# Low-rank expert matrices of the last stage: all eight experts' factors against the two chosen ones fetched by index

## What is computed

```python
def _gates(cls_tok, Wr):
    logits = cls_tok @ Wr.T
    top_vals, top_idx = jax.lax.top_k(logits, K)          # K = 2 of E = 8
    ...
    return jax.nn.softmax(masked, axis=-1)
gates = _gates(x[:, 0, :], Wr)
mid = jnp.einsum('blh,erh->belr', x, A)                   # A: 8 x 64 x 256
expert_out = jnp.einsum('belr,ehr->belh', mid, Bw)        # Bw: 8 x 256 x 64
weighted = jnp.einsum('be,belh->blh', gates, expert_out)
return x + weighted
```

## Time and profile before

| | before |
|---|---|
| median of 3 runs | 502.54 us (502.24 to 504.96) |
| the profiled execution, its own time | 502.1 us |
| its span in the trace | 500.3 us |
| TensorE busy in the span | 471.9 us, 94% |
| VectorE, ScalarE, GpSimd busy | 285.4, 202.6, 234.0 us |
| 480 to 490 us of the span: TensorE busy | 10.00 of 10.00 us |
| 490 to 501 us: TensorE busy | 6.95 of 11.00 us |
| granted TensorE clock, 440 us to the end | 1.00 |

### The profile page before, as it was taken

How to read it: one execution, slowest core, us unless ns; L and a number is a source line. 1 busy time by engine, 2 the same in 40 slices (tenths; PEclk the granted TensorE clock), 3 DMA queues, 4 the chain that set the end, 5 groups by cost and what they waited for, 6 DMA issues and landing times.

```text
span 500.3 us, 9491 instructions
## 1 busy us (share of the span) xinstructions
PE 471.9 (94%) x3132; PEld 387.1 (77%) x3132; DVE 285.4 (57%) x656; ACT 202.6 (40%) x453; POOL 234.0 (47%) x312
## 2 busy tenths in 40 slices
PE   6899999798999999989999999999977999899897
PEld 5677776575777787769999999999965777677686
DVE  3879985642263122345555545454564689998733
ACT  3455774556620021002323232323323666665640
POOL 3523344044237566129985643333327655662350
PEclk9999999998999999999999999999997999999999
DMA  8999300020002224999223323221129100000004
GB/s 275 363 427 362 27 12 1 1 85 2 0 1 89 89 90 129 333 331 309 45 61 97 105 86 86 66 86 54 43 88 315 41 0 1 1 3 1 1 23 146
DMA packets 48879, 53.51 MB, mean 107 GB/s; under 512 B 15265, under 2 KB 43234, under 8 KB 48578
## 3 DMA queue, kind: packets, MB, share of 16 engines
q1 hardware_dynamic: 35890, 24.33, 17.4%
q0 software_dynamic: 7424, 19.67, 11.6%
q10 hardware_dynamic: 5520, 8.91, 5.9%
HBM read 35.78 MB, written 17.12 MB: 106 GB/s over the span
## 4 chain that ended last, share of the span: by engine, by line
PE 77%; DVE 12%; ACT 4%; DMA 3%; issue 2%; ACTq 1%; POOL 1%; SPq 0%; POOLq 0%
PE banks L1212 10%; PE banks L1262 9%; PE banks L1314 5%; PE banks L347 5%; PE banks L325 5%; PE banks L361 5%; PE banks L1315 5%; PE banks L1318 5%; PE banks L314 3%; DVE mx L503 3%; PE banks L1336 3%; PE banks L1337 3%; PE banks L1340 3%; PE banks L1728 3%; PE banks L1326 3%; DVE ps L506 2%
## 5 line engine op out<-in xcount | busy, mean ns | idle before, releaser
L116 POOL TENSOR_TENSOR rstd<-var,mhalf 128x2 f32<-128x2 f32 x30 | 21.0, 698 | 92.8 <-DVE var L109 92.8
L1142 ACT ACTIVATE hg<-banks 128x352 f32<-128x352 f32 x39 | 18.1, 465 | 96.6 <-PE banks L1318 91.8
L1314 PE MATMUL banks<-w_hi,xgT_hi 128*128 x156 | 54.8, 352 | 2.0 <-ACT xgT_hi L949 1.9
L1487 DVE TENSOR_TENSOR hgT_lo<-banks,hgT_hi 128x256 fp32r<-128x256 f32 x78 | 24.1, 351 | 56.2 <-ACT hgT_hi L1149 56.2
L503 DVE TENSOR_REDUCE mx<-banks 128x16 f32<-128x1024 f32 x32 | 39.0, 1220 | 24.5 <-PE banks L325 24.4
L1315 PE MATMUL banks<-wd,xgT_hi 128*128 x156 | 50.3, 324 | 0.0
L1262 PE MATMUL banks<-sdn,big 128*128 128x256 f32 x192 | 47.5, 393 | 0.0
L1262 PEld LDWEIGHTS banks<-sdn,big 128*128 128x128 f32 x192 | 34.1, 189 | 12.6 <-issue 9.0
L325 PE MATMUL banks<-kvb,qT 64*128 64x256 f32 x256 | 37.6, 414 | 4.0 <-DVE ps L506 2.9
L1046 POOL DMA_INDIRECT expert_rows_in<-xn,slot x32 | 31.5, 986 | 18.3 <-issue 7.6
L1318 PE MATMUL banks<-w_hi,xgT_lo 128*128 x156 | 37.6, 322 | 0.0
(11 more groups left out here) (244 smaller groups left out, 1140.3 us busy)
## 6 DMA issues: line engine op xcount, KB each, us to landing
w_hi<-in_egu POOLq DMA_DIRECT2D x2, 2816.0 KB, 21.1
expert_rows_in<-zeros SPq DMA_DIRECT2D x1, 5304.0 KB, 40.0
xn<-expert_rows_in SPq DMA_DIRECT2D x39, 128.0 KB, 2.0
y_all<-choices_out SPq DMA_DIRECT2D x16, 256.0 KB, 5.5
wd<-in_egu ACTq DMA_DIRECT2D x8, 352.0 KB, 9.5
wd<-in_egu ACTq DMA_DIRECT2D x4, 704.0 KB, 13.5
out_x<-x SPq DMA_DIRECT2D x8, 256.0 KB, 2.1
x<-in_x SPq DMA_DIRECT2D x2, 896.0 KB, 8.1
```

Source lines behind the costliest of these rows:

```text
L1314: nc.tensor.matmul(to, xgT_hi[:, c, k, :], hi, start=(k == 0), stop=False)
```

## The change

The factors are no longer loaded whole. `choose` works out, for each of 128 partitions, a row number: partitions 0 to 63 hold the 64 rows of the first chosen expert, partitions 64 to 127 those of the second (`kmax` is 8 minus the expert's number, so the row is 512 - 64 * `kmax` + the partition's place in its half). GpSimd then fetches these rows of both factors for each batch by four indirect DMAs. The gates need only two halves of one column. With 128 rows in place of 512, a batch's matrix takes 2 matmuls and its weighting one instruction. The order is changed too: both weightings and both matrices stand at slot 16 with the first unit's product, both `keep_matrix` stand right behind `inverse(7)` on ScalarE, and `turn3(5)` comes after `project_o(7)`.

```diff
 def top_two(nc, dve, sem, base, p, rev, work, shape, low):
-    key, top1, hot1, rest, top2, hot2, kmax = work
+    key, top1, hot1, rest, top2, hot2, kmax1, kmax2 = work
...
-    for src, top, hot in ((p, top1, hot1), (rest, top2, hot2)):
+    for src, top, hot, kmax in ((p, top1, hot1, kmax1), (rest, top2, hot2, kmax2)):
...
-        fa = space("fa", KR * D).rearrange("p (k n) -> p k n", k=KR)
-        fb = space("fb", KR * D).rearrange("p (k n) -> p k n", k=KR)
-        fbg = space("fbg", B * KR * D).rearrange("p (b k n) -> p b k n", b=B, k=KR)
+        fa, fb, fbg = [space(n, B * D).rearrange("p (b n) -> p b n", b=B) for n in ("fa", "fb", "fbg")]
...
-            nc.tensor.wait_ge(ffn1_in, 48)
+            nc.tensor.wait_ge(ffn1_in, 16)
...
             v.tensor_tensor(gc["d"][:, :], gc["top2"][:, :], gc["top1"][:, :], ALU.subtract).then_inc(f_g, 1)
+            nc.vector.wait_ge(f_rows, 2)
+            for q, kmax in enumerate(("kmax1", "kmax2")):
+                half = slice(q * R, (q + 1) * R)
+                link(v.scalar_tensor_tensor(gc["row"][half, :], gc[kmax][half, :], -float(R), first_row[half, :], ALU.mult, ALU.add))
+            v.tensor_copy(picked[:, :], gc["row"][:, :]).then_inc(f_rows, 1)
...
             link(v.reciprocal(gc["inv"][:, :], gc["den"][:, :]))
-            wide = lambda a: a.unsqueeze(2).to_broadcast([P, B, E])
-            link(v.tensor_tensor(gt["gate"][:, :, :], gt["hot2"][:, :, :], wide(gc["e"][:, :]), ALU.mult))
-            link(v.tensor_tensor(gt["gate"][:, :, :], gt["gate"][:, :, :], gt["hot1"][:, :, :], ALU.add))
-            link(v.tensor_tensor(gt["gate"][:, :, :], gt["gate"][:, :, :], wide(gc["inv"][:, :]), ALU.mult))
-            for b in range(B):
-                pairs = gt["gate"][:, b, :].rearrange("p (k q) -> p k q", q=2)
-                for q in range(2):
-                    v.tensor_copy(gcol[q * R:(q + 1) * R, b, :], pairs[q * R:(q + 1) * R, :, q]).then_inc(f_gcol, 1)
+            v.tensor_copy(gcol[0:R, :], gc["inv"][0:R, :]).then_inc(f_gcol, 1)
+            v.tensor_tensor(gcol[R:2 * R, :], gc["inv"][R:2 * R, :], gc["e"][R:2 * R, :], ALU.mult).then_inc(f_gcol, 1)
+
+        def first_rows():
+            nc.gpsimd.iota(first_row[:, :], [[0, B]], base=E * R, channel_multiplier=1,
+                           allow_small_or_imprecise_dtypes=True).then_inc(f_rows, 1)
+
+        def second_half_rows():
+            nc.vector.wait_ge(f_rows, 1)
+            v.tensor_scalar(first_row[R:2 * R, :], first_row[R:2 * R, :], -float(R), None, ALU.add).then_inc(f_rows, 1)
+
+        def pick_factors(b):
+            nc.gpsimd.wait_ge(f_rows, 3)
+            for to, table in ((fa, a_in), (fb, bw_in)):
+                nc.gpsimd.indirect_dma_start(to[:, b, :], None, table[:, :],
+                                             bass.IndirectOffsetOnAxis(ap=picked[:, b:b + 1], axis=0),
+                                             bounds_check=E * R - 1).then_inc(f_picked[b], 16)
 
         def weigh_second_factor(b):
-            nc.scalar.wait_ge(f_gcol, 2 * B)
-            nc.scalar.wait_ge(ffn1_in, 48)
-            for k in range(KR):
-                nc.scalar.activation(fbg[:, b, k, :], fb[:, k, :], ACT.Copy, scale=gcol[:, b, k:k + 1]).then_inc(f_scaled, 1)
+            nc.scalar.wait_ge(f_gcol, 2)
+            nc.scalar.wait_ge(f_picked[b], 32)
+            nc.scalar.activation(fbg[:, b, :], fb[:, b, :], ACT.Copy, scale=gcol[:, b:b + 1]).then_inc(f_scaled, 1)
 
         def batch_matrix(b):
-            nc.tensor.wait_ge(f_scaled, (b + 1) * KR)
+            nc.tensor.wait_ge(f_scaled, b + 1)
             wait(nc.tensor, events1["sub_done"], 2 * NU)
             for m in range(KD):
-                for k in range(KR):
-                    last = nc.tensor.matmul(MATRIX_IN[b][:, m * D:(m + 1) * D], fa[:, k, m * P:(m + 1) * P],
-                                            fbg[:, b, k, :], start=(k == 0), stop=(k == KR - 1))
+                last = nc.tensor.matmul(MATRIX_IN[b][:, m * D:(m + 1) * D], fa[:, b, m * P:(m + 1) * P],
+                                        fbg[:, b, :], start=True, stop=True)
             last.then_inc(f_w, 1)
...
             sp.dma_start(wr[:, :, :], split(wr_in)).then_inc(ffn1_in, 16)
-            sp.dma_start(fa, a_in.rearrange("(k p) n -> p k n", p=P)).then_inc(ffn1_in, 16)
-            sp.dma_start(fb, bw_in.rearrange("(k p) n -> p k n", p=P)).then_inc(ffn1_in, 16)
...
-                       16: lambda: (batch_matrix(0), turn3(5)),
-                       "end": lambda: (batch_matrix(1), product3(0), turn3(6), product3(1), product3(2), product3(3),
-                                       turn3(7), product3(4), product3(5), product3(6), product3(7)),
+                       16: lambda: (batch_matrix(0), batch_matrix(1), product3(0)),
+                       "end": lambda: (turn3(5), product3(1), product3(2), turn3(6), product3(3), product3(4),
+                                       turn3(7), product3(5), product3(6), product3(7)),
...
-                       16: lambda: weigh_second_factor(0),
-                       "end": lambda: (weigh_second_factor(1), copy3(4), normalise3(5), keep_matrix(0), copy3(5),
-                                       normalise3(6), keep_matrix(1), copy3(6), normalise3(7), copy3(7))}
+                       16: lambda: (weigh_second_factor(0), weigh_second_factor(1)),
+                       "end": lambda: (keep_matrix(0), keep_matrix(1), copy3(4), normalise3(5), copy3(5),
+                                       normalise3(6), copy3(6), normalise3(7), copy3(7))}
...
```

More of the change, by code:

```diff
@@ L42 @@
 R = 64
-KR = E * R // P
 EP = E + 2
@@ L1421, in vector_on @@
                         (hot["key"][:, :, :], tag[:, 0, :, 0], hot["hot1"][:, :, :], hot["rest"][:, :, :],
-                         tag[:, 1, :, 0], hot["hot2"][:, :, :], col["kmax"][:, :]), [P, NT, E], -2.0)
+                         tag[:, 1, :, 0], hot["hot2"][:, :, :], col["kmax"][:, :], col["kmax"][:, :]), [P, NT, E], -2.0)
             v.tensor_tensor(hot["mask"][:, :, :], hot["hot1"][:, :, :], hot["hot2"][:, :, :], ALU.add).then_inc(masked, 1)
@@ L1554, in xattn_ffn_kernel @@
         wr = sb("wr", [P, KD, E])
-        gt = {n: sb("gt_" + n, [P, B, E]) for n in ("p", "key", "hot1", "rest", "hot2", "gate")}
-        gc = {n: sb("gc_" + n, [P, B]) for n in ("top1", "top2", "kmax", "d", "e", "den", "inv", "nmean", "var", "rstd", "shift")}
-        gcol = sb("gcol", [P, B, KR])
+        gt = {n: sb("gt_" + n, [P, B, E]) for n in ("p", "key", "hot1", "rest", "hot2")}
+        gc = {n: sb("gc_" + n, [P, B]) for n in ("top1", "top2", "kmax1", "kmax2", "row", "d", "e", "den", "inv", "nmean", "var",
+                                                 "rstd", "shift")}
+        gcol = sb("gcol", [P, B])
+        first_row, picked = sb("first_row", [P, B]), sb("picked", [P, B], I32)
+        f_rows, f_picked = sem("f_rows"), [sem(f"f_picked{b}") for b in range(B)]
         g_stats, g_mv = sb("g_stats", [1, B, 6]), sb("g_mv", [1, B, 2])
@@ L1780, in xattn_ffn_kernel @@
                        14: lambda: normalise3(3), "inverse7": gate_exp, "exps7": lambda: (copy3(3), normalise3(4)),
-                       16: lambda: weigh_second_factor(0),
-                       "end": lambda: (weigh_second_factor(1), copy3(4), normalise3(5), keep_matrix(0), copy3(5),
-                                       normalise3(6), keep_matrix(1), copy3(6), normalise3(7), copy3(7))}
-        vector_work = {6: lambda: stats3(0), 8: lambda: (row_stats(), stats3(1)), 9: row_norm, 10: lambda: stats3(2),
+                       16: lambda: (weigh_second_factor(0), weigh_second_factor(1)),
+                       "end": lambda: (keep_matrix(0), keep_matrix(1), copy3(4), normalise3(5), copy3(5),
+                                       normalise3(6), copy3(6), normalise3(7), copy3(7))}
+        vector_work = {6: lambda: stats3(0), 8: lambda: (row_stats(), stats3(1)), 9: lambda: (row_norm(), second_half_rows()), 10: lambda: stats3(2),
                        11: spread_columns, 12: lambda: stats3(3), 13: choose, 14: lambda: stats3(4), 15: gates,
@@ L1787, in xattn_ffn_kernel @@
                        "end": lambda: (stats3(7), *(add3(u) for u in range(NU)))}
-        gpsimd_work = {7: lambda: rstd3(0), 8: row_rstd, 9: lambda: rstd3(1), 11: lambda: (rstd3(2), add_norm(0)),
-                       13: lambda: (rstd3(3), add_norm(1)), 15: lambda: (rstd3(4), add_norm(2)),
+        gpsimd_work = {7: lambda: (rstd3(0), first_rows()), 8: row_rstd, 9: lambda: rstd3(1), 11: lambda: (rstd3(2), add_norm(0)),
+                       13: lambda: (rstd3(3), add_norm(1)), 15: lambda: (rstd3(4), pick_factors(0), pick_factors(1), add_norm(2)),
                        16: lambda: (rstd3(5), add_norm(3), rstd3(6), add_norm(4), rstd3(7),
```

2 lines of the change are left out of this document (1 added, 1 removed).

## The result

| | before | after |
|---|---|---|
| median of 20 runs each | 503.86 us (501.21 to 507.44) | 498.49 us (496.31 to 502.57) |
| ratio, 95% interval | | 0.9902 [0.9881, 0.9923] |
| the profiled execution, own time / span | 502.1 / 500.3 us | 499.5 / 497.4 us |
| mean granted TensorE clock in it | | 0.985 |

The kernel is faster by 1.0%. The forecast range, 495.6 to 498.9, holds the median, 0.4 us from its upper end, and 9 of the 20 runs lie above it. So two things have to be explained apart: what the last stage gained, and why the level is off.

A forecast was written before the change was run, and what follows sets the result against it. The prediction took the last stage as bound by TensorE's own work plus one stall. -6.22 there and +0.50 in `choose` gave -5.72, so 502.1 became 496.4 us, range 495.6 to 498.9.

The forecast's parts named there:

- What bounds the kernel: Last stage: bound by TensorE's own work, with one stall ahead while TensorE waits for the normalised unit 5.
- The loads go, 0: SyncE's queue: removing two 512 KB factor loads changes nothing, taken as 0; any gain bounded by 1.2 us.
- The iota, `second_half_rows`, shorter `gates`, 0: GpSimd slot 7, VectorE slot 9 and near 468.5: small additions and some 0.8 us saved, all hidden, taken as 0.
- Three instructions in `choose`, +0.50: VectorE ahead of `mx`: two linked steps at 0.21 and a copy at 0.08 on the path, bounds 0.3 to 0.8.
- Four indirect DMAs with 0.6 us of slack: GpSimd behind `rstd3(4)`: rows land 2.6 us after issue, weighted by 471.9, before `inverse(7)` at 472.54; 0 on the path.
- The rival of late rows: Fetch on GpSimd: landing of 4.4 us gives 497.6, of 5.5 gives 498.7; chance 0.12.
- TensorE's piece, -6.22: End of `values(7)` to last product: 24.94 us becomes 18.72; 5.17 from removed matmuls, 1.05 from the stall and its neighbours.
- The port rival: `ninv` of unit 6 on VectorE waits 0.5 to 0.98 us for a pick: 496.9 to 497.4; chance 0.12.
- The other two rivals: Fetch landing: 7.4 us gives 500.6, no difference (0.04); over 11.4 us, gather not spread over DMA engines, slower (0.04).
- The level and the width of the range: Whole kernel: sum taken from the profiled execution's 502.1 us, with 0.5 us allowed for the spread of executions.
- The first rival: Whole kernel: the sum holds, 496.4 us, own range 495.8 to 497.0; chance 0.68.
- The time around the span: Outside the profiled span: 1.8 us between span 500.3 and own time 502.1, carried over unchanged.

The follow-up runs named there:

- kernel 8: Changed kernel with both 512 KB loads of all factors still issued into memory that nothing reads: 498.13 us, ratio 0.9885.
- kernel 7: Changed kernel with a shorter `choose`: second comparison and copy removed, row numbers written as integers at once, halves not linked: 497.88 us, one run.
- Kernel 5: Changed kernel with `add_norm(2)` put ahead of the four indirect DMAs on GpSimd: 497.90 us, one run.
- kernel 6: Changed kernel with fixed rows loaded by four plain DMAs in place of the fetch by index: 498.44 us, one run.
- kernel 9: Changed kernel with a shorter `choose`, one full-height instruction making all row numbers, and both `fb` fetches first: 498.49 us, ratio 0.9889.
- kernel 2: Changed kernel again, with only a harmless maximum with 0 added on an expert number: 500.75 us, ratio 0.9888.
- kernel 10: Changed kernel a third time, with only the harmless maximum added, on another chip: 497.55 us, ratio 0.9895.
- Kernel 4: Kernel before, with 512 rows and no fetch by index, given the new TensorE and ScalarE order: 506.87 us, ratio 0.9986.
- kernel 3: Changed kernel with fetched rows but the TensorE and ScalarE order of the kernel before: 503.85 us, ratio 0.9935.
- kernel 1: Kernel before again, with only a harmless maximum with 0 added on an expert number: 507.07 us, ratio 0.9988.

## Why the prediction was wrong, and what in it was right

The forecast is 2.1 us under the median, and 503.86 - 502.1 = 1.8 of them are the base that the sum was taken from: that base, and the spread allowed around it, is the step that failed. The rest is the gain: 5.72 us were forecast and 5.37 lie between the two medians. The parts, in the order of the prediction:

**What bounds the kernel: right.** TensorE's own work set the end of the last stage, before and after; the sum was made on the right engine.

**The loads go, 0: right** (kernel 8). **The iota, `second_half_rows`, shorter `gates`, 0:** nothing between `mx` and the end of `values(7)` grew (-0.05).

**Three instructions in `choose`, +0.50: right,** +0.45 measured: 0.37 for the two halves and 0.08 for the copy. That the link sets the pitch of the halves is not shown; without it (kernel 7) it is the same.

**Four indirect DMAs with 0.6 us of slack: wrong, at no price.** The last one started at 471.86 in an execution 2.59 us late, that is at 469.3 against the forecast 468.8; the issue ahead of the first is 0.62 and not 0.30, the pitch from first to second 1.45. The landing took 2.84 in place of 2.6. Together 0.7 us against 0.6: the slack was gone. Kernel 5 shows that the next 0.76 us come onto the path in full, kernel 6 that in the changed kernel itself no more than 0.05 does. I called 3.2 us of landing the edge; with these starts the edge was at about 2.75 (475.03 - 0.42 - 471.86). The rival of late rows had more for it than its 0.12.

**TensorE's piece, -6.22: right in kind, 0.32 too good.** The mis-sized terms are the two places where TensorE turns to new work behind `values(7)`, priced like work in a row. The chain has the matrices at 1.93 (forecast 1.73 and a wait of 0.1) and the first product, behind the wait for `keep_matrix(0)`, at 1.96 (1.73). That makes 0.33, the whole of the difference. For a piece behind a wait had a sign: the transposes behind the stall take 0.66 where those in a row take 0.44. For the matrices a wait is not the reason: kernels 6 and 9, whose weighted rows were there long before, have the same 1.92. In before the first matrix opens the same way (a first record of 483 ns where the median is 379), hidden there by the stall behind it. What costs the 0.1 us at that place is open.

**The port rival: refuted.** `ninv` beside an indirect DMA takes 0.70 in the changed kernel, and in kernels 2, 8, 9 and 10. The rule of the Trainium skill, page "SBUF — State Buffer", section "SBUF: two separate sides", has a VectorE instruction with two SBUF inputs and a GpSimd instruction that reads SBUF lock each other out. The trace doesn't agree with it for an indirect DMA, though the earlier trace rows agree for a GpSimd addition. **The other two rivals,** no difference and slower, needed landings of 7.4 and over 11.4 us; it was 2.8.

**The level and the width of the range: wrong, and this is the step that failed.** The local sum was 0.22 us off, the median 2.1. I set the sum against one execution of 502.1 us, and gave "0.5 us for the spread of executions". But 20 runs of before lie between 501.21 and 507.44 with their median at 503.86, 1.8 above that execution, and the three runs shown already reached 504.96. That the median still lies in the range of 495.6 to 498.9 is luck: its upper end was put there for a pick on the port and for rows that land late, and neither cost anything to speak of. The first rival's own range, 495.8 to 497.0, holds 3 of the 20 runs. (Its lower end was also added up 0.1 too low: 496.4 - 0.2 - 0.5 is 495.7.)

**The time around the span, 1.8 us in both kernels: wrong, 0.3 too low.** It was carried over without a reason. In the runs that list their span it is 1.7 to 1.8 us in the kernel before and 2.0 to 2.2 in the changed kernel. Kernel 4 (order alone) has before's 1.7 to 1.8, kernels 3 and 8 have the changed kernel's 2.1, and so has the single run of kernel 6, which fetches nothing by index; kernel 9 has 1.9. So it came with the 128 row form of the kernel and not with the order, the removed loads or, as far as one run tells, the picks; the cause is open. Less this, the 5.50 us of T are 5.1 in the time of an execution, against 5.37 between the medians, whose interval reaches from 3.9 to 6.0.

How the time follows the clock is seen in the 20 runs of the changed kernel: spans of 494.2 to 495.9 at a mean granted clock of 0.993, 495.1 to 497.0 at 0.989, 496.8 to 499.9 at 0.985 to 0.986, and 500.5 at 0.979. In all sets of six runs or more the correlation is between -0.76 and -0.98, with 3.2 to 5.1 us for 0.01 of mean clock. On the chip of kernels 5 to 10 four runs of before at 0.993 have spans of 500.0 to 500.7, and four of kernels 8 and 10 have 494.5 to 495.1: their means lie 5.5 us apart, as T says. So the local gain is in the span. The forecast 496.4 is the time of an execution with little lost to the clock: the two runs next to it (496.31 and 496.43) had 0.993, and 14 of the 20 had 0.990 or less. The chip adds to the level too: at 0.990 the median span of before is 504.6 on the chip of kernels 1 to 4 and 501.8 beside kernels 9 and 10. That the clock goes with the time is shown; why a dip comes in one execution and not in the next is open, as is what makes up the 2 us or so by which runs of one chip and equal clock still differ.

## What to carry to other kernels

Measure a local edit by an interval inside the trace whose two ends hang on each other by waits, and read the total only for the level; here the interval repeats within 0.03 us where the total scatters by 6. Check apart what lies outside the span; here it grew by some 0.35 us. Take the level and the width of a forecast from the scatter of all runs shown, not from the one that was profiled, and price a TensorE piece behind a wait or at the head of new work by rows of such pieces, not by rows from the middle of a stream. Shortening work and reordering it belong together: the work made short exposed a stall (2.18 us) which only the new order took away.

## What the runs showed of the hardware

- An indirect gather of 128 rows of 1 KB lands 2.8 to 2.9 us after its instruction starts on GpSimd (changed kernel; up to 3.5 in kernel 5); four in a row have a pitch of 1.31 to 1.45 us, and the first one behind other work has 0.62 us of issue ahead of it where the next have 0.30.
- An indirect DMA does not hold up a two-input VectorE instruction beside it (0.70 against 0.69 us, in five kernels).
- Two VectorE instructions over 64 partitions each, on different halves and with no link between them, don't overlap (kernel 7: 0.34 us for both, the next start 0.37 after the first), while unlinked ones over 128 partitions start 0.07 to 0.08 apart (kernel 9).
- The granted TensorE clock can fall to its lower level for about 3 us right behind two idle times of 1 us (kernel 4, 1.55 us on one projection) where the same instructions at the same place kept the upper level in other executions.
